# Four-layer graph network on one core: the order of four VectorE comparisons in each slot of the first layer's edge loop

## The reference, cut to what matters

```
edge_index = stack([src, dst])
h = maximum(layernorm(x), 0)
x = x + L0(h, edge_index, edge_attr_16, ...)   # attention: softmax over the edges of a destination
  g      = leaky_relu(xl[src] + xr[dst] + edge_attr @ W_e)
  logits = einsum('ehc,hc->eh', g, att)
  alpha  = softmax of logits over the edges with the same dst
  out    = segment_sum(xl[src] * alpha, dst)
x = x + L1(relu(layernorm(x)), ...)            # 4 steps of segment_sum(emb[col], row)
x = x + L2(...);  x = x + L3(...)              # a message layer and a 2-hop propagation
```

## Time and profile before

| what | value |
|---|---|
| three runs, median | 8474.16 us |
| three runs, lowest and highest | 8428.90 us, 8522.11 us |
| the profiled execution's own time | 8382.76 us |
| its span in the trace | 8380.9 us |
| share of the span busy: PE, PEld, DVE, ACT, POOL | 63%, 52%, 37%, 22%, 45% |

### The profile page before, as it was taken

The page is one execution under the profiler, slowest core; times in us unless marked ns, Lnnn a source line. Parts: engine busy times, 40 slices in busy tenths (PEclk is TensorE's granted clock), DMA queues, the critical chain, the costliest instruction groups (busy, mean ns, idle before and its releaser), DMA issues. The chain is left out here.

```text
span 8380.9 us, 115433 instructions
## 1 busy us (share of the span) xinstructions
PE 5284.0 (63%) x35142; PEld 4387.9 (52%) x35142; DVE 3126.2 (37%) x3916; ACT 1807.6 (22%) x3844; POOL 3796.8 (45%) x3496
## 2 busy tenths in 40 slices
PE   0133767766776777667329994666666666665398
PEld 0122544444444445444229993666566665564298
DVE  3584555555555656555262212111111111111421
ACT  0002333433333434333100000222222221221000
POOL 0365445554554656555400004665566566565200
PEclk9856777777777777777559995555555555555699
DMA  6103343333343434434229983555455454453396
GB/s 264 37 19 96 102 110 102 114 102 109 107 113 99 119 106 122 114 104 113 51 97 366 366 305 108 177 162 170 154 162 175 158 169 158 152 162 103 118 391 261
DMA packets 661030, 1260.27 MB, mean 150 GB/s; under 512 B 173453, under 2 KB 467662, under 8 KB 635160
## 3 DMA queue, kind: packets, MB, share of 16 engines
q1 hardware_dynamic: 382552, 725.95, 25.2%
q10 hardware_dynamic: 166656, 412.78, 14.5%
q0 software_dynamic: 111424, 117.64, 7.0%
HBM read 926.24 MB, written 487.07 MB: 169 GB/s over the span
## 5 line engine op out<-in xcount | busy, mean ns | idle before, releaser
L563 POOL DMA_INDIRECT att_gl<-tab_l,att_ix x1568 | 1817.0, 1159 | 1474.4 <-DVE att_msg L715 990.8
L1050 POOL DMA_INDIRECT sum_gl<-tab_l,sum_ixs x1568 | 1543.8, 985 | 1042.6 <-DVE sum_t L970 500.4
L804 ACT ACTIVATE att_acc<-att_pc 128x392 bf16<-128x392 f32 x2352 | 1093.6, 496 | 1892.5 <-PE att_pc L582 913.9
L582 PE MATMUL att_pc<-att_acc,att_ohv 128*128 128x392 bf16 x2352 | 928.0, 395 | 603.7 <-issue 331.5
L579 PE MATMUL att_pc<-att_ohl,att_ohv 128*128 128x392 bf16 x2352 | 936.8, 398 | 146.2 <-DVE att_ohl L678 146.2
L970 DVE TENSOR_TENSOR sum_t<-sum_pb,sum_gl 128x512 f32<-128x512 f32 x196 | 135.3, 690 | 2203.7 <-remote 1524.3
L1000 PE MATMUL sum_pm<-sum_msg,sum_S 128*128 128x64 f32 x3136 | 682.2, 417 | 260.3 <-ACT sum_msg L1024 260.3
L1000 PEld LDWEIGHTS sum_pm<-sum_msg,sum_S 128*128 128x128 f32 x3136 | 664.0, 326 | 283.6 <-ACT sum_msg L1024 233.6
L582 PEld LDWEIGHTS att_pc<-att_acc,att_ohv 128*128 128x128 bf16 x2352 | 253.5, 108 | 1040.3 <-ACT att_acc L804 524.4
L620 PE MATMUL att_pm<-att_msg,att_S 128*128 128x69 f32 x3136 | 597.5, 348 | 304.5 <-issue 236.3
L598 PEld LDWEIGHTS att_pl<-att_xe,att_S 128*128 128x128 f32 x3136 | 659.9, 234 | 172.6 <-issue 148.5
(11 more groups left out here) (310 smaller groups left out, 5450.8 us busy)
## 6 DMA issues: line engine op xcount, KB each, us to landing
A<-att_acc SPq DMA_DIRECT2D x2352, 98.0 KB
l_a<-A SPq DMA_DIRECT2D x147, 1568.0 KB, 8.8
l_at<-AT SPq DMA_DIRECT2D x98, 1568.0 KB, 8.3
att_dall<-in_dst ACTq DMA_DIRECT2D x224, 448.0 KB
sum_dall<-in_dst SPq DMA_DIRECT2D x196, 512.0 KB
sum_a<-A SPq DMA_DIRECT2D x49, 1568.0 KB
AT<-sum_at ACTq DMA_DIRECT2D x49, 1568.0 KB
tot<-att_o ACTq DMA_DIRECT2D x56, 1022.0 KB, 4.2
```

What stands on the lines that cost most here:

```text
L563: nc.gpsimd.indirect_dma_start(out=gl[s][:, c, :], out_offset=None, in_=g.tab_l, in_offset=bass.IndirectOffsetOnAxis(ap=ix[s][:, c:c + 1], ...
L582: nc.tensor.matmul(pc[c][m % 2][:, 0:LO], ohv[c][h][:, m, :, 1], acc[c][(t * CJ + m - 1) % CR][:, :], start=False, stop=True).then_inc(s_m ...
L804: nc.scalar.activation(acc[c][n % CR][:, :], pc[c][m % 2][:, 0:LO], ACT.Copy).then_inc(s_acc[c], 1)
L1050: nc.gpsimd.indirect_dma_start(out=gl[q][:, j, :], out_offset=None, in_=g.tab_l, in_offset=bass.IndirectOffsetOnAxis(ap=ixs[q][:, j:j + 1] ...
```

## The change

In each slot VectorE made row one-hots and low parts of chain 0, then both of chain 1. Now it makes the low parts of both chains, then the row one-hots of both. The four instructions, their sizes and their operands stay the same; the wait for a chain's buffers (`s_mm[c]`) stands ahead of its low parts now. Each chain's semaphore still counts two.

```
-                def items(i, t, c):
+                def items(i, t):
                     h = t % 2
-                    n0 = i * (CB * CJ) + (c * CI + t * CJ)
-                    if not known(i, 1) or t >= 2:
-                        dve.wait_ge(s_mm[c], i * (CB * CJ) + ((t - 1) * CJ if t >= 2 else -t * CJ))
-                    v.tensor_tensor(ohv[c][h][:, :, :, :], ...row one-hots..., ALU.is_equal).then_inc(s_oh[c], 1)
-                    v.tensor_tensor(ohl[c][h][:, :, :, :], ...low parts..., ALU.is_equal).then_inc(s_oh[c], 1)
+                    n0 = [i * (CB * CJ) + (c * CI + t * CJ) for c in range(CH)]
+                    for c in range(CH):
+                        if not known(i, 1) or t >= 2:
+                            dve.wait_ge(s_mm[c], i * (CB * CJ) + ((t - 1) * CJ if t >= 2 else -t * CJ))
+                        v.tensor_tensor(ohl[c][h][:, :, :, :], ...low parts..., ALU.is_equal).then_inc(s_oh[c], 1)
+                    for c in range(CH):
+                        v.tensor_tensor(ohv[c][h][:, :, :, :], ...row one-hots..., ALU.is_equal).then_inc(s_oh[c], 1)
...
                         if t < CB:
-                            for c in range(CH):
-                                items(i, t, c)
+                            items(i, t)
```

More of the change, by code:

```diff
@@ L668, in same @@
                                     ALU.is_equal).then_inc(s_S, 1)
-                def items(i, t, c):
+                def items(i, t):
                     h = t % 2
-                    n0 = i * (CB * CJ) + (c * CI + t * CJ)
-                    if not known(i, 1) or t >= 2:
-                        dve.wait_ge(s_mm[c], i * (CB * CJ) + ((t - 1) * CJ if t >= 2 else -t * CJ))
[L675 to L680, removed]
+                    n0 = [i * (CB * CJ) + (c * CI + t * CJ) for c in range(CH)]
+                    for c in range(CH):
+                        if not known(i, 1) or t >= 2:
+                            dve.wait_ge(s_mm[c], i * (CB * CJ) + ((t - 1) * CJ if t >= 2 else -t * CJ))
+                        v.tensor_tensor(ohl[c][h][:, :, :, :], spread(c_lo2[:, :, :].unsqueeze(1), [P, CJ // 2, LO, 2]),
+                                        spread(g.lo[:, bass.ds(n0[c], CJ)].rearrange("p (j two) -> p j two", two=2)
+                                               .unsqueeze(2), [P, CJ // 2, LO, 2]), ALU.is_equal).then_inc(s_oh[c], 1)
+                    for c in range(CH):
+                        v.tensor_tensor(ohv[c][h][:, :, :, :], spread(c_row2[:, :, :].unsqueeze(1), [P, CJ, P, 2]),
+                                        spread(g.vals[:, bass.ds(n0[c], CJ), :].unsqueeze(2), [P, CJ, P, 2]),
+                                        ALU.is_equal).then_inc(s_oh[c], 1)
                 def logits(i, n, b, s, k):
```

## The result

| | median (us) | runs | ratio to before, 95% interval |
|---|---|---|---|
| before | 8451.53 | 8428.57 to 8522.11 (4) | |
| after | 8823.35 | 8800.0 to 8842.83 (4) | 1.0424 [1.0352, 1.0496] |

The account below looks back on a forecast made before the run. No engine was full: the edge loop alternated between POOL's gathers, during which SyncE, ScalarE and TensorE crawl, and messages steps. Only POOL's held time counted, 48 us: 8474 - 48 = 8426 us, range 8340 to 8560.

Parts of the forecast that it names:

- Part 1: VectorE's four one-hot instructions: same length, 4.32 us, in either order; the moved buffer wait is already over; no cost.
- Part 2: TensorE: chain 0 ready 1.16 us later, hidden by the wait for chain 1; cost nothing, at most 32 us.
- Chain 0's delay shows: Rival: TensorE's cover fails in slot 3 every turn, 32 us, POOL's time worth nothing; 8506 us, chance 0.08.
- Part 3: POOL's gathers beside the quad: held 0.72 us instead of 1.92, 87 quads, up to 104 us less busy time.
- the let-in rule: POOL: a gather arriving during a VectorE instruction is held until that gives way to the next, then takes 0.90 us.
- What 104 us of POOL time is worth: Edge loop: 48 us gained, from 40 quads where TensorE waits anyway at 1.20 us each; 0 for the other 47.
- The freeze comes earlier: Rival: denser gathers move ScalarE's second copy in slot 3 behind a gap, 22 x 4.12 = 91 us; 8565 us, chance 0.14.
- All of it: Rival: each gather costs the chain a fixed stretch, so POOL's 104 us are won in full; 8370 us, chance 0.25.
- Nothing: Rival: work between messages steps sets the pace, POOL only waits longer; no change, 8474 us, chance 0.17.

Follow-up runs that it names:

- chain0_third: Kernel before with the quad ordered row one-hots 1, low parts 0, row one-hots 0, low parts 1: 8479.05 us, ratio 0.9969; on a faster chip 7019.37 us, 0.9999.
- the second pair of traces: Kernel before and changed kernel traced again, both unchanged; before against itself 1.0007; POOL's gathers 1786.8 us before, 1600.2 us after.
- chain_lo_first: Kernel before with the quad ordered low parts 0, row one-hots 0, low parts 1, row one-hots 1: 8707.36 us, 1.0241; on a faster chip 6911.16 us, 0.9844.

## Why the prediction was wrong

It said 8426 us, 8340 to 8560; the time is 8823, above the range and with the other sign.

- **Part 1**, a quad of the same length and waits that are over: held. In slot 3 the quad takes 4.33 us from its start to that of what follows (2656.76 to 2661.09), against 4.32 forecast.
- **Part 2**, TensorE pays nothing for chain 0's delay: held, but for a slip in its sum. The third of the four instructions starts at X + 2.58 and takes 0.95, so chain 0 is ready at X + 3.53, 1.28 us later than before, not at X + 3.40, 1.16 later. With the 0.05 us to the first product of the earlier trace rows that is X + 3.58; X + 3.59 was measured, against X + 3.46 forecast. Nothing hung on it: chain 1 unmoved at X + 4.46, TensorE's wait for the quad not longer, and `chain0_third` equal to before. *Chain 0's delay shows* is out.
- **Part 3**, the let-in rule: held, to 0.05 us, in orders that the trace of before doesn't have. A port let go only behind the whole quad is excluded by the same rows: three gathers end inside it. Its total was mis-sized, 219 us for 104 (187 in the second pair of traces). The count was short: the trace of before has 101 such pairs that start 1.20 us into a quad, not 87, which makes 121 us. The rest is argued and not measured: with the chain frozen fewer VectorE instructions fall into phases at all, so it would be the freeze's doing and not a gain.
- **What 104 us of POOL time is worth** is the step that failed. Its term was a gain of 48 us, from "nothing is lost by letting a gather through" in the 40 quads in which TensorE waits anyway, and 0 for the other 47. In its place the medians show a loss of 372 us. I took the rates inside and outside a phase, 0.48 and 1.19 copies per us, as given, and asked only how many us would go. The rate inside isn't fixed: it depends on how closely the gathers come, which is what the change alters. It fell from 19.6 copies in 40.8 us to 8.0 in 36.9. That may feed on itself, by the reading of the traces and not by a run: a frozen chain gives VectorE nothing to do, so nothing holds the gathers, and they stay 1.25 us apart. But a freeze need not last to the end of the phase, as the stop that ended at 2603.62 shows.
- ***The freeze comes earlier*** was the right rival in kind, at 0.14. Its price was one gap of 4.12 us in 22 quads, 91 us; 372 were measured. Its deciding point was wrong too: in the slot 3 shown chain 1's copy still came at X + 5.39. The loss lay later, in slots 0 and 3, by some 9 to 11 us a turn each. I had taken the one gap of the earlier trace rows for the size of a freeze, although shows a phase of 37 us with six instructions of ScalarE. That row held the price: a phase that came to look like it, with 4 copies where the mean has 20, would lose 16 / 1.19 = 13 us, and all 56 so 750 us, as an upper bound. The 372 measured are half of that; which half, the row couldn't tell.
- *All of it* and *Nothing* shared the error, a chain whose pace doesn't depend on how closely the gathers come. The case in which all of it is won exists, on the 7020 chips: `chain_lo_first` gains 1.6% there for a smaller cut in held time. The changed kernel itself was not run on one of them, so whether it is faster there is open.

**Open** are also: why the signal that TensorE's products are done reaches ScalarE and VectorE so late while gathers come closely; where between 1.25 and 1.63 us that ends; and why chips differ in it. One rival stands untested: the recording. Each time here comes with a span and a granted clock, so with records of its execution, and on the 8500 chips these records are incomplete. The same kernel, `chain0_third`, left 56866 semaphore updates in its trace on an 8500 chip and 116044 on a 7020 chip. Whether the freeze would be there in an execution that nobody records, no run here shows.

## What to carry to other kernels

An engine's pauses can be what lets the others work: before freeing an engine that isn't the bound, ask whether the rate of the rest holds when it has no pauses, and price the bad case by the worst stretch in the trace, not by the mildest. Where bursts of indirect gathers alternate with waits for their users, try pacing them before making them denser. Time on more than one chip: here the same order of four instructions was worth -1.6% on one and +2.4% on another.

## What the runs showed of the hardware

- While POOL issued gathers of 128 rows each 1.25 us apart, ScalarE and VectorE saw TensorE's products done only 17 and 21 us after these had ended by the records, and TensorE and SyncE's transfers stood with them (2611.45 to 2624.95 in `after`); with the gathers 1.63 us apart that was gone (ratio 0.9283), though POOL was then busy 90% of a stretch of 100 us.
- The same kernel took 8450 to 8524 us on some chips and 7016 to 7021 on others. On the latter POOL waited 12 us for messages in `chain0_third`'s loop, against 1158 for the same kernel on the former.
- A held gather gets in where one VectorE instruction gives way to the next, even if the two are of one kind and overlap in the records: the gather of 2606.05 ends at 2607.03, 0.90 us behind 2606.13, where by the 1.29 us of the earlier trace rows the second `ohl` starts, and that of 2607.34 at 2608.33, 0.90 us behind the start of the `ohv` pair (2607.43). The Trainium skill, in "SBUF — State Buffer", section "SBUF: two separate sides", has the loser of the shared port blocked for the whole of the other's instruction; for a held gather the trace agrees, instruction by instruction. The other way round it doesn't show it: the quad beside three gathers takes its 4.33 us, and no VectorE instruction of it waits for one.
